# One head's complex product split between VectorE and GpSimd, bf16 weight copies dropped, gate logits computed apart

## The reference

```python
q  = (LN(x) @ W_q.T)  split in 16 heads of 128
kv = (LN(x) @ W_kv.T) split in 16 heads of 128
qf, kvf = fft(q), fft(kv), each divided by its l2 norm
kvf = cumsum(kvf, axis=rows)
values = real(ifft(qf * kvf))
x1 = x + LN(values @ W_o.T)
h = LN(x1)
logits = h @ gate_w.T + gate_b          # 8 experts, the best 2 taken
xA = h @ lora_A.T                       # 8 experts x rank 16 = 128 columns
out = x1 + LN(h @ W.T + b + sum over the 2 of gate * (xA @ lora_B.T))
```

## Time and profile before

| | |
|---|---|
| median of 3 runs | 1653.82 us (1653.64 to 1655.4) |
| the profiled execution | 1657.21 us |
| its span, slowest core (core 6) | 1655.7 us (cores from 1641.4 us) |
| busy in it: PE, DVE, ACT, POOL | 1284.9, 698.6, 444.4, 95.8 us |
| mean granted TensorE clock, core 6 | 0.868 of full speed |

### The profile page before, as it was taken

One profiled execution on the slowest core, in us unless ns is written; L12 is line 12 of the kernel. 1 busy time (PEld: TensorE's weight loads), 2 busy tenths in 40 slices (PEclk: granted clock), 3 DMA queues, 4 the chain that ended last, 5 costly groups with the idle time before them and its releaser, 6 DMA issues. The chain is left out here.

```text
span 1655.7 us, 15368 instructions; the slowest of 8 cores (1641.4 to 1655.7 us)
## 1 busy us (share of the span) xinstructions
PE 1284.9 (78%) x5664; PEld 536.5 (32%) x5664; DVE 698.6 (42%) x977; ACT 444.4 (27%) x442; POOL 95.8 (6%) x186
## 2 busy tenths in 40 slices
PE   2479999979999974666666648999937788898785
PEld 2334444433444430111111113444413344444332
DVE  3500000000000016999999932444434555455553
ACT  3401101101111025666666610000002323323321
POOL 1100000000000003000000020111110000000000
PEclk9999999989999995666666659999978888888987
DMA  6622122112122107998000045444440121121121
GB/s 104 105 38 39 28 37 38 26 26 39 26 39 38 26 14 89 103 114 102 1 0 1 0 127 153 115 115 115 115 128 13 64 77 59 57 77 62 54 77 51
DMA packets 22801, 102.98 MB, mean 62 GB/s; under 512 B 3376, under 2 KB 3512, under 8 KB 20168
## 3 DMA queue, kind: packets, MB, share of 16 engines
q0 software_dynamic: 22112, 101.76, 29.9%
q1 hardware_dynamic: 616, 0.23, 0.1%
HBM read 128.24 MB, written 41.94 MB: 103 GB/s over the span
## 5 line engine op out<-in xcount | busy, mean ns | idle before, releaser
L310 PE MATMUL PMAIN<-AR,OV 128*128 128x512 bf16 x2048 | 457.8, 382 | 37.5 <-ACT AR L336 13.6
L310 PEld LDWEIGHTS PMAIN<-AR,OV 128*128 128x128 bf16 x2048 | 197.3, 98 | 298.4 <-issue 74.5
L349 DVE TENSOR_TENSOR OV<-AR 128x2048 bf16<-128x2048 bf16 x32 | 39.2, 1225 | 491.3 <-ACT AR L339 491.3
L856 PE MATMUL PAUX<-AR 128*128 128x512 bf16 x1024 | 233.8, 391 | 0.0
L431 ACT ACTIVATE AR<-PAUX 128x1024 bf16<-128x1024 f32 x128 | 124.0, 1021 | 75.1 <-DVE AR L511 42.6
L336 ACT ACTIVATE AR<-PMAIN 128x1024 bf16<-128x1024 f32 x32 | 32.7, 1023 | 414.5 <-PE PMAIN L310 414.5
L856 PEld LDWEIGHTS PAUX<-AR 128*128 128x128 bf16 x1024 | 101.3, 100 | 126.3 <-issue 13.6
L585 PE MATMUL PMAIN<-AR 128*128 128x512 bf16 x512 | 116.9, 390 | 19.1 <-DMA AR<-wotb_s 19.1
L585 PE MATMUL PAUX<-AR 128*128 128x512 bf16 x512 | 111.8, 379 | 0.0
L478 PE MATMUL PAUX<-AR,MSIN 128*128 128x512 bf16 x128 | 56.5, 563 | 54.5 <-ACT AR L431 54.5
L478 PE MATMUL PAUX<-AR,CMAT 128*128 128x512 bf16 x128 | 50.5, 500 | 38.4 <-DVE AR L522 21.8
(11 more groups left out here) (116 smaller groups left out, 1151.2 us busy)
## 6 DMA issues: line engine op xcount, KB each, us to landing
AR<-x POOLq DMA_DIRECT2D x32, 512.0 KB, 5.4
out<-AR POOLq DMA_DIRECT2D x16, 1024.0 KB, 5.1
OV<-wqs POOLq DMA_DIRECT2D x16, 512.0 KB, 5.0
OV<-wkvs POOLq DMA_DIRECT2D x16, 512.0 KB, 5.0
wotb_s<-wot POOLq DMA_DIRECT2D x16, 512.0 KB, 40.7
wtb_s<-wt POOLq DMA_DIRECT2D x16, 512.0 KB, 110.3
AR<-wotb_s POOLq DMA_DIRECT2D x16, 512.0 KB, 14.3
x1s<-AR POOLq DMA_DIRECT2D x16, 512.0 KB, 2.9
```

The source lines that it names most:

```text
L310: ins = te.matmul(PMAIN[:, nn * 512:(nn + 1) * 512], lhsT, XCT[:, c * 2048 + nn * 512: c * 2048 + (nn + 1) * 512], start=(c == 0), stop=(c ...
L349: v.tensor_mul(SQ[h % 2], DEST[:, h * 2048:(h + 1) * 2048], DEST[:, h * 2048:(h + 1) * 2048]).then_inc(s_sq, 1)
L856: te.matmul(PAUX[:, nn * 512:(nn + 1) * 512], lhsT, WTB[:, c * 2048 + nn * 512: c * 2048 + (nn + 1) * 512], start=(c == 0), stop=False)
```

## The change

It has three parts.

1. In b2 GpSimd computes two of the four products of a head, QF_RE*KVC_RE and QF_IM*KVC_IM, into buffers of its own (`T1G`, `T2G`). VectorE computes the other two, then the sum, then waits for GpSimd (`s_gprod`) and forms the difference. ScalarE's putting out of QF for the next head and VectorE's next scans wait for the same semaphore.
2. The 32 copies to bf16 in DRAM and the two DRAM tensors are gone. WOTB and WTB are loaded from the f32 tensors, and the DMA casts on its way.
3. The one product with 136 columns becomes two, with 8 (gate, `GWTB`, into `PLG`) and with 128 columns (lora_A, `ABTB`, into `PXA`), in turns chunk by chunk. VectorE waits for `s_xamm` before it weights xA. There is one small load more, of the gate's weights.

```diff
-    AGWB = OV1[:, 1024:3200]
+    ABTB = OV1[:, 2048:4096]
+    GWTB = nc.alloc_sbuf_tensor("GWTB", [HD, HD], BF16)
...
-        @blk.gpsimd
-        def _(g):
-            for c in range(NCH):
-                g.dma_start(wotb_d.ap()[c * 128:(c + 1) * 128, :],
-                            wot_d.ap()[c * 128:(c + 1) * 128, :]
-                            ).then_inc(s_pcast, 16)
...
                     if j == 8 and h >= 1:
                         a.wait_ge(s_cm, h)
+                        a.wait_ge(s_gprod, h)
...
+        @blk.gpsimd
+        def _(g):
+            for hh in range(NH):
+                g.wait_ge(s_scand, hh + 1)
+                g.wait_ge(s_fa, 6 * hh + 6)
+                g.wait_ge(s_fb, 6 * hh + 6)
+                if hh >= 2:
+                    g.wait_ge(s_cm, hh - 1)
+                g.tensor_tensor(T1G, QF_RE, KVC_RE, ALU.mult)
+                g.tensor_tensor(T2G, QF_IM, KVC_IM, ALU.mult
+                                ).then_inc(s_gprod, 1)
...
             def midsec_a(v, h):
+                if h >= 1:
+                    v.wait_ge(s_gprod, h)
...
             def midsec_b(v, h):
-                v.tensor_mul(T1, QF_RE, KVC_RE)
-                v.tensor_mul(T2, QF_IM, KVC_IM)
-                v.drain()
-                v.wait_ge(s_ifft, h)
-                v.tensor_sub(QV_RE, T1, T2)
-                v.drain()
                 v.tensor_mul(T1, QF_RE, KVC_IM)
                 v.tensor_mul(T2, QF_IM, KVC_RE)
                 v.drain()
-                v.tensor_add(QV_IM, T1, T2).then_inc(s_cm, 1)
+                v.wait_ge(s_ifft, h)
+                v.tensor_add(QV_IM, T1, T2)
+                v.drain()
+                v.wait_ge(s_gprod, h + 1)
+                v.tensor_sub(QV_RE, T1G, T2G).then_inc(s_cm, 1)
                 v.drain()
...
-            g.wait_ge(s_pcast, 16 * 2 * NCH)
             for c in range(NCH):
                 g.dma_start(WOTB[:, c * 2048:(c + 1) * 2048],
-                            wotb_d.ap()[c * 128:(c + 1) * 128, :]
+                            wot_d.ap()[c * 128:(c + 1) * 128, :]
...
                 g.dma_start(WTB[:, c * 2048:(c + 1) * 2048],
-                            wtb_d.ap()[c * 128:(c + 1) * 128, :]
+                            wt_d.ap()[c * 128:(c + 1) * 128, :]
...
                 for c in range(NCH):
                     lhsT = L3TD[t % 2][:, c * 128:(c + 1) * 128]
-                    te.matmul(PXAG, lhsT, AGWB[:, c * 136:(c + 1) * 136],
+                    te.matmul(PLG, lhsT, GWTB[:, c * 8:(c + 1) * 8],
                               start=(c == 0), stop=False)
-                te.matmul(PXAG, SELS[:, 0:128], GB16[:, :],
+                    ins = te.matmul(PXA, lhsT, ABTB[:, c * 128:(c + 1) * 128],
+                                    start=(c == 0), stop=(c == NCH - 1))
+                    if c == NCH - 1:
+                        ins.then_inc(s_xamm, 1)
+                te.matmul(PLG, SELS[:, 0:128], GB16[:, :],
                           start=False, stop=True).then_inc(s_gmm, 1)
```

## The result

The changed kernel takes 1752.5 us (median), the kernel before in the same sessions 1654.5: ratio 1.0579, 95% interval 1.0564 to 1.0594, so +96 us. Forecast were 1767 us and +113. Faster than forecast by 15 us, well inside the range, and the cause of most of it, turns between the two engines in b2, is the one named.

What follows compares the result with a forecast made beforehand. VectorE was taken to set the pace in b2, TensorE in c, a chain over several engines in d. 83 + 20.5 + 2.6 + 3 + 4 = +113 us on 1654 gave 1767 us, range 1660 to 1815.

Steps and rivals of the forecast that it cites:

- Turns in b2: In b2 VectorE and GpSimd take turns, a head taking 25.5 us against 20.49; +83 us, 1767 us in all, 62%.
- Rival B: In b2 the engines run side by side, P about 4.4 us, 19.2 us a head; 1664 us in all, 13%.
- C: In b2 the engines run side by side with P under 3.83 us, a faster kernel; 1645 us, 8%.
- D: In b2 GpSimd is slower than the scan, P about 6 us; by turns 1818 us, side by side about 1717; 17%.
- P: Time of one GpSimd product of 2048 columns in b2, taken as 4.42 us from the scan.
- The size of b2: Block b2 grows by 70 us in 14 heads and 13 us in the first and last, +83 us.
- The rival on the other side: In b2 GpSimd works beside VectorE, as 16 undelayed issues suggested: 1664 us at 13%, or 1645 us at 8%.
- Casting loads in c: In c the 16 WOT loads take 2.90 us each instead of 1.62, covered by nothing; +20.5 us.
- The first x1s load: In d the last two casting chunks stand in the queue ahead of this load, on the chain; +2.6 us.
- The gates apart: In d 16 added matmuls with weight loads cost 1.1 to 1.9 us a tile, mostly covered; +3 and +4 us.
- The +3 for the end tiles: In d's first and last tile the added matmuls are on the chain, +1.5 us each.
- The +4 for the tiles between: In d's 14 middle tiles TensorE's slack covers most of the added matmuls, leaving 0.3 us a tile.

Runs made afterwards that it cites:

- PSUM operand: Kernel before with two products a head on GpSimd, and VectorE's four small products taking one factor from PSUM instead of SBUF; ratio 1.0215.
- memsets: Kernel before with six GpSimd memsets of 2048 columns added per head in b2, nobody waiting for them; 1656.0 us.
- part 2 alone: Kernel before with only the bf16 DRAM copies removed and WOT and WT loaded with a cast; ratio 1.0172, +28 us.
- free products: Kernel before with two GpSimd products per head added on unchanging q data, no other engine waiting for them; ratio 1.0622, +103 us.

## Why the prediction was right, step by step

- **The total** was closer than its terms. Against the blocks' lengths b2 was forecast 17 us too long (+83, measured +65.7), c 5 us too short (+20.5, +25.6) and d 5 us too long (2.6 + 3 + 4 = +9.6, +4.5); the last two cancel by luck.
- **Turns in b2** (the forecast, 62%): right, and shown from three sides: by no wait at all (+103 us), by write-only work (nothing), by a PSUM operand (small products untouched). Rival B, side by side, with 19.2 us a head, and C fell with the first timeline; D, a slow GpSimd, fell with P: 4.05 us unheld, 4.43 and 4.49 with GpSimd's own waiting in it. That 4.42, taken from the scan, comes so close is in part luck: the scan was only the nearest row.
- **The size of b2** was +83 us forecast, +66 measured, the largest error of the sum. The head is 24.40 us and not 25.5. From the end of the scans (822.64) to L505 (832.92) it is 10.28 us and not 0.2 + 8.84 + 2.5 = 11.5. The term that was too large is P, as a time that is to be added to VectorE's: unheld it is 4.05 us, and twice the 0.37 between is 0.7 of the 1.26 us. The rest, 0.5 us, isn't resolved here. The forecast's 1.1 us too many a head make some 17 us in 16 heads, the whole difference.
- **The rival on the other side** rested on GpSimd's issues in b2 that nobody held. They were weak evidence, twice over. In 4.66 of the 7.64 us VectorE was idle, so few of the 16 issues lay beside any work of it. And they are not reading tiles, which is what holds VectorE: the memsets, which don't either, go through beside it in the same way. What an issue does to SBUF no run here shows; the stretched ones of the first block stay unexplained.
- **Casting loads in c**: +20.5 forecast, +25.6 measured (+26.9 alone). The step, nothing covers them, holds; the rate taken for them was a little high (2.90 us a chunk, measured 3.1) and the one before a little low (1.62, measured 1.55). In groups of four chunks the rate of bytes read is the same before and after: 2.1 MB of bf16 in 6.2 us and 4.2 MB of f32 in 12.4 us are both 338 GB/s.
- **The first x1s load**: +2.6 forecast; with part 2 alone d grew by 2.6 us and the load by 2.5 (8.2 to 10.7), in the changed kernel the load by 3.5.
- **The gates apart**: +7 forecast, +8 (5 to 11) measured alone, and here the size came out right by luck, for both of its terms failed. The +3 for the end tiles took the price of an added matmul with its weight load to be that of one of 136 columns; it is 0.3 us for all 16, and the end tiles grew by 0.4. The +4 for the tiles between was to come from TensorE's slack; they grew by 5.9 through the x1s load. In the changed kernel the same part costs next to nothing: d grew by 4.5 us, 2.6 of which part 2 gives alone.

The Trainium skill (SBUF — State Buffer, Who interferes with whom) says that a VectorE instruction with two SBUF inputs contends with a GpSimd instruction that reads SBUF and not with one that only writes it, and that one with at most one SBUF input outside the two-port modes does not contend. All of it agrees with the free products (+103 us), the memsets (+0) and the PSUM operand (1.2 us each, unheld). Its "fully blocks" and "for the whole instruction" stand in the entry on VectorE's two-port modes; the two-input instructions here behave so too: beside the scans a held instruction lasts the other's time and about its own (8.31 us where the two alone take 4.05 and 4.42). The Trainium skill (GPSIMD Engine Reference, Elementwise — side-by-side cycle accounting) gives 4497 ns for two fp32 inputs of 2048 columns; for bf16 the traces here have 4.05 us where GpSimd is not held and 4.4 to 4.5 us in the changed kernel's head, GpSimd's waiting included.

## What to carry to other kernels

Before work is moved from VectorE to GpSimd, look at what both read: if VectorE's instructions in that stretch have two SBUF operands and GpSimd's read SBUF at all, the two take turns, and the move costs GpSimd's time less VectorE's and hides nothing but the idle time that VectorE had there (1.4 us a head here). Look for it in stretched instructions, not in idle time. At a block's start look at what the first tile's loads wait for; a buffer that the block before empties piece by piece can take them early, and that was worth 20 us here, where each split of the arithmetic that was tried cost time.

## What the runs showed of the hardware

- A scan whose second input is one zero per partition, read 2048 times, is held by GpSimd's reading like a product of two full tiles (8.31 us instead of 4.42), and holds GpSimd in turn (8.16 instead of 4.05). In the pair that starts together, the product, 0.02 us ahead, goes through unheld in 4.05 us.
- The DRAM to DRAM casts at 113 GB/s written read twice that, 339 GB/s together, the same total as the loads of either kind (338 GB/s read). In c a cast from f32 costs its f32 bytes. That one limit on DRAM's bytes stands behind all three is inferred from these figures; no run varied it.
- GpSimd takes 1.79 us for a memset of 2048 bf16 columns, 1.89 for a copy and 4.05 for a product where nothing holds it; with VectorE's turns between it is 2.3 us from start to start for copies and 4.4 for products.
- Sixteen matmuls of 8 columns, each with its weight load, put in turns between sixteen of 128 columns, cost TensorE 0.3 us in all, at either level of the clock (2.44 against 2.12 us at 1.2 GHz, 1.55 against 1.26 at 2.4, compared with sixteen of 136 columns).
